# Distance attention on one Trainium2 core: who spreads the first two tiles of keys of a new pair of batches

## The reference, cut to what matters

```
q, k, v = (x @ W.T + b).reshape(B, S, 16, 8)          # B=8, S=512
distance = pos_q[:, None] - pos_q[None, :]
pos_emb = dist_emb[MAX_POS - 1 + distance]
scores  = einsum('bqhd,bkhd->bhqk', q, k) / sqrt(8)
scores += einsum('bqhd,qkd->bhqk', q, pos_emb)
scores += einsum('bkhd,qkd->bhqk', k, pos_emb)
ctx = einsum('bhqk,bkhd->bqhd', softmax(scores), v)
```

## Time and profile before

| | |
|---|---|
| median of 3 runs | 4081.83 us (4081.24 to 4086.81) |
| the profiled execution | 4118.69 us, its span 4117.0 us |
| distance attention in the profile | about 2570 to 3750 us of the span |
| PE busy | 3405.0 us (83%) |
| DVE busy | 3335.7 us (81%) |
| ACT busy | 2876.1 us (70%) |
| POOL busy | 1125.8 us (27%) |

### The profile page before, as it was taken

The page is one execution under the profiler, slowest core; times in us unless marked ns, Lnnn a source line. Parts: engine busy times, 40 slices in busy tenths (PEclk is TensorE's granted clock), DMA queues, the critical chain, the costliest instruction groups (busy, mean ns, idle before and its releaser), DMA issues. The chain is left out here.

```text
span 4117.0 us, 71499 instructions
## 1 busy us (share of the span) xinstructions
PE 3405.0 (83%) x27092; PEld 2097.7 (51%) x27092; DVE 3335.7 (81%) x4520; ACT 2876.1 (70%) x2433; POOL 1125.8 (27%) x983
## 2 busy tenths in 40 slices
PE   3899999999999999999947963688988898898890
PEld 2233333333333333333335861587887887887790
DVE  7999999999999999999937445668777787876662
ACT  3999999999999999999903323466666675664430
POOL 2121111221122111112100543534333334330235
PEclk8899999999999999999977986799999999997995
DMA  5000000000000000000031224411213113111022
GB/s 157 7 13 6 13 13 6 13 13 13 6 13 13 6 13 13 6 13 13 5 107 67 56 56 139 97 25 33 39 25 48 31 25 54 18 25 68 26 63 67
DMA packets 237595, 146.44 MB, mean 36 GB/s; under 512 B 147105, under 2 KB 220417, under 8 KB 236833
## 3 DMA queue, kind: packets, MB, share of 16 engines
q1 hardware_dynamic: 228640, 125.03, 12.6%
q0 software_dynamic: 8704, 17.84, 1.8%
HBM read 90.73 MB, written 52.10 MB: 35 GB/s over the span
## 5 line engine op out<-in xcount | busy, mean ns | idle before, releaser
L698 PE MATMUL psA<-wave,diag 128*128 128x512 f32 x3072 | 1439.9, 620 | 137.5 <-DVE score L854 89.4
L766 ACT ACTIVATE wave<-wave 128x2048 f32<-128x2048 int32 x640 | 1181.1, 1904 | 3.5 <-DVE wave L841 2.1
L698 PEld LDWEIGHTS psA<-wave,diag 128*128 128x128 f32 x3072 | 582.3, 196 | 895.5 <-issue 696.8
L635 POOL TENSOR_TENSOR diag<-ident,par 128x128 f32<-128x128 f32 x384 | 291.6, 785 | 1422.7 <-PE psA L698 1422.7
L816 DVE TENSOR_SCALAR wave<-s,par 128x2048 int32<-128x2048 int32 x480 | 611.1, 1273 | 0.0
L841 DVE TENSOR_SCALAR wave<-wave 128x2048 int32<-128x2048 int32 x512 | 608.4, 1212 | 0.0
L1729 POOL COPY kb<-ks 48x1024 bf16<-48x1024 bf16 x160 | 319.0, 1994 | 570.4 <-PE psR L1789 380.7
L1870 ACT COPY r<-psR 128x1024 f32<-128x1024 f32 x320 | 310.9, 1026 | 155.0 <-PE psR L1789 154.9
L731 ACT ACTIVATE s<-psS,par 128x1024 int32<-128x1024 f32 x256 | 282.6, 1104 | 121.9 <-PE psS L661 121.9
L854 DVE SCALAR_TENSOR_TENSOR score<-wave,par,psA 128x1024 f32<-128x1024 f32 x256 | 317.3, 1269 | 36.9 <-PE psA L698 36.9
L1879 ACT ACTIVATE W<-psR 128x1024 f32<-128x1024 f32 x256 | 249.4, 1024 | 132.3 <-PE psR L1814 132.3
(11 more groups left out here) (259 smaller groups left out, 4461.5 us busy)
## 6 DMA issues: line engine op xcount, KB each, us to landing
ks<-kb_parts SPq DMA_DIRECT2D x56, 384.0 KB, 6.2
qs<-qb_parts SPq DMA_DIRECT2D x32, 384.0 KB, 6.2
ys<-f_ys SPq DMA_DIRECT2D x36, 256.0 KB
wave_out<-og SPq DMA_DIRECT2D x33, 256.0 KB, 2.1
o<-wave_out SPq DMA_DIRECT2D x8, 1024.0 KB, 5.2
qp<-qa_parts SPq DMA_DIRECT2D x32, 192.0 KB, 3.5
kp<-ka_parts SPq DMA_DIRECT2D x32, 192.0 KB, 4.0
f_wu<-in_w_up SPq DMA_DIRECT2D x2, 2048.0 KB, 9.5
```

The lines of the kernel that those rows point to most:

```text
L635: ins = pool.tensor_tensor(diag[:, h % 2, f, :], ident[:], par[:, u, 1, h * NF + f:h * NF + f + 1] .to_broadcast((P, P)), ALU.mult)
L698: mm = pe.matmul(psA[:, kt, :], diag[:, h % 2, f, :], wave[:, h % 2, f, kt * L:(kt + 1) * L], start=(f == 0), stop=(f == PE_F - 1), skip_g ...
L766: act.activation(wave[:, h % 2, f, :], angle[:, h % 2, f, :], ACT.Sin, scale=float(TWO_PI / 2.0 ** 32)).then_inc(sine, 1)
```

## The change

At the three boundaries the keys of the first two units (u = 16, 17, 32, 33, 48, 49) are no longer spread by POOL. They leave `spread_steps`, and with it `k_order`. Instead ACT copies one quarter of the tile behind each of eight exponentials of the last query tile of the old pair: keys of the first unit behind e2, e3, e4, e5, keys of the second behind e8, e9, e10, e11. Ahead of the first quarter of each tile ACT waits for the tile's transfer and for the last r2 that read the buffer. PE waits on a new semaphore for these tiles. All other spreads stay on POOL, four copies each as before, only written through the common helper `quarter`.

```diff
-                for v in (u + QT, u + QT + 1):
-                    if v in k_spreads:
-                        yield "k", v
...
+    new_keys = [u for u in range(QT * QT, NU) if u % (QT * QT) < 2]
+    quarters = {(u // QT - 1, 2 + 6 * (u % QT) + n): (u, n) for u in new_keys for n in range(4)}
...
+        new_kb_ready = sem(c, "new_kb_ready")
...
+        def quarter(dst, src, n):
+            half, odd = divmod(n, 2)
+            pairs = slice(half * PAIRS // 2, (half + 1) * PAIRS // 2)
+            rows = slice(odd * ODD, odd * ODD + NR)
+            return (dst[rows, pairs, odd, :],
+                    src[rows, :, :].rearrange("r h (n two) -> r n h two", two=2)[:, pairs, :, odd])
...
-                    if u in k_spreads and k % 2 == 0:
+                    if u in new_keys and k % 2 == 0:
+                        pe.wait_ge(new_kb_ready, 4 * new_keys.index(u) + k + 2)
+                    elif u in k_spreads and k % 2 == 0:
                         pe.wait_ge(kb_ready, 4 * k_order.index(u) + k + 2)
...
+            def spread_new(u, n):
+                if n == 0:
+                    act.wait_ge(ks_loaded[ks_of(u)], 32 * k_landed(u))
+                    act.wait_ge(filled, fill["r2", k_spreads[u], CH - 1] + 1)
+                act.copy(*quarter(kb[:, kb_of(u), :, :, :], ks[:, ks_of(u), :, :], n)).then_inc(new_kb_ready, 1)
...
                 elif kind == "e":
                     weigh(i, k)
+                    if (i, k) in quarters:
+                        spread_new(*quarters[i, k])
```

More of the change, by code:

```diff
@@ L1723, in _ @@
         def _(pool):
[L1725 to L1732, removed]
             def spread_q(q):
@@ L1738, in spread_q @@
                         pool.wait_ge(filled, fill["r1", q * QT - 1, 2 * half + 1] + 1)
-                    spread(qb, qs[:, q % 2, :, :], half, qb_ready)
+                    for n in (2 * half, 2 * half + 1):
+                        pool.tensor_copy(*quarter(qb, qs[:, q % 2, :, :], n)).then_inc(qb_ready, 1)
             def spread_k(u):
@@ L1744, in spread_k @@
                     pool.wait_ge(filled, fill["r2", k_spreads[u], CH - 1] + 1)
-                for half in range(2):
-                    spread(kb[:, kb_of(u), :, :, :], ks[:, ks_of(u), :, :], half, kb_ready)
+                for n in range(4):
+                    pool.tensor_copy(*quarter(kb[:, kb_of(u), :, :, :], ks[:, ks_of(u), :, :], n)).then_inc(kb_ready, 1)
             pool.memset(kb[:, 0, :, :, :], 0.0).then_inc(zeroed, 1)
```

## The result

The changed kernel is slower. Over 18 runs its median is 4095.29 us (4083.51 to 4106.44) against 4083.07 us (4074.29 to 4093.75) for the kernel before; the ratio is 1.003, with a 95% interval from 1.0021 to 1.0038. I had said 4058.8 us, 0.57% faster. The two whole spans of the profiles (4117.0 us before, 4090.0 us now) say nothing on the change: the profiled execution of the kernel before took 4118.69 us, 35.6 us over that median, and outside the distance attention it was 31.7 us longer than the profiled one of the changed kernel. I compare boundary tiles, from one spread of queries to the next.

A forecast was written before the change was run, and what follows sets the result against it. DVE's subtractions under POOL's copies were taken to set the boundary tiles' time. 3 x (-10.44 regained + 2.75 for ACT's quarters) = -23.1 us off the median of 4081.8 gave 4058.8 us, range 4050 to 4070.

The forecast's parts named there:

- e8: Exponential on ACT, filled by PE beforehand; the second tile's first quarter follows it, and the layout starts it at 2742.36.
- e11: Exponential on ACT, filled by PE beforehand; the second tile's last quarter follows it, and the layout starts it at 2749.38.
- The price of a quarter: One strided key copy on ACT: 0.95 us taken, lower bound 0.9, upper bound POOL's 1.99 for the same pattern.
- Idle time, ring and hand-over: ACT's 3.52 us idle in the first tile, the ring's room before PE's e7, and 0.2 us from ACT to PE.
- the layout: ACT's row laid out anew with the quarters, against PE's fill times; at 0.95 us a quarter r2[3] starts 2.75 us late.
- e7: PE's fill for an exponential, where the first tile's cost was read: 0 as forecast, 2.7 us at 2.0 us a quarter.
- In short: 4 quarters less 1.05 us of slack. After that nothing is later: Second tile's cost on PE: r2[3] 2.75 us late, all that follows moving by the same amount.
- e13: PE's fill for an exponential, waiting for ACT to take e11; forecast to start 1.73 us late.
- e14: PE's fill for an exponential after r2[3]; forecast as ready, with no lateness beyond that of r2[3].
- e15: PE's last fill for an exponential in the unit, after e14; forecast with no lateness beyond that of r2[3].
- The sum at 2.0 us: Both tiles' costs together if a quarter takes 2.0 us: 10.6 us a boundary.
- The rival: Strided read on ACT: at 1.99 us a quarter costs eat the gain, slower by over 0.2% from 2.33; chance 0.04.

The follow-up runs named there:

- The probe: Changed kernel plus a block behind the distance attention where ACT, POOL and DVE each make the same 48 x 1024 copy in several forms; 4270.06 us, single run.
- the second tile alone: Changed kernel with only ACT's four quarters for the second tile, the first unit's new keys never spread; ratio 0.9975 to the kernel before.
- The runs with one tile: Changed kernel with ACT's four quarters for only the first or only the second tile, the other never spread; ratios 0.996 and 0.9975 to the kernel before.

## Why the prediction was wrong, step by step

- **What bounds the boundary tiles: right.** POOL's copies stretched DVE's subtractions. With the copies gone the mean is 480 ns, and the tiles without any spread of new keys were 32.3 us shorter, where I had 31.3 from the subtractions alone and 3.3 of clock as perhaps.
- **The price of a quarter: wrong, and it decides.** The step that failed is "I take 0.95 us for a quarter". It took 2.00, over the 1.2 us that I had named as the sign of being wrong. I priced by the engine, from a stepped read of PSUM and a contiguous read of SBUF, and put POOL's 1.99 us for the very same pattern at the far end as if it were a slow engine's. The second of these rows was no support at all: 1904 - 1026 = 878, and 1904 less 878 gives back the 1026 that I had put in. The probe shows that ACT and POOL cost nearly the same for the same pattern (1.91 and 1.88 us), and that the step of the read in SBUF makes both 1.8 times as dear. Of the rows that I had, the one with the same operands was the nearest.
- **Idle time, ring and hand-over: right at their price.** At 1.04 us a quarter PE was 3.4 us late where the layout gives 3.1, and the kernel was 19.0 (medians) to 20.8 us (ratio) faster where I had said 23.1. At 2.0 us the first tile cost 3.7 us and not 2.7, since I stopped at e7 and ACT, still full, held e8 as well.
- **"In short: 4 quarters less 1.05 us of slack. After that nothing is later": wrong at the real price.** The text priced a wait of PE at its length. At 2 us a quarter PE is busy 2.2 of the 5 us around e13 and r2[3], its clock falls to 0.50, and it does r2[3], v5 and some or all of e14 and e15 at about half pace: 2.6 us at the first boundary of the changed kernel, 2.0 at the second, 2.9 with the second tile alone. The stall of the kernel before had a low clock too (0.65 and 0.67 from 2870 to 2880 us), but there PE was waiting for DVE in any case.
- **The sum at 2.0 us: wrong by itself.** The text has 10.6 us a boundary, but its own terms give 2.7 + (8.0 - 1.05) = 9.65 us (and 6.15, not 6.6, at 1.5 us). The runs with one tile give 3.7 us for the first, 0.7 more where the clock falls behind e7, and 7.0 for the second; with the 2.6 us at the end that is 14.0 of the 14.1 us measured. That the 10.6 lay near 3.7 + 7.0 was luck.
- **The rival.** At 1.99 us I had the costs "eat the gain", with a loss beyond 0.2% only from 2.33 us on. With the lower clock the point of decision lies lower: at 2.00 us the kernel is 0.3% slower. Without it the two tiles would by this sum have cost 10.7 us, about what DVE got back, so the price of the quarter ate the gain and the clock made the loss. The mechanism of that rival is what happened; its chance of 0.04 and its threshold were wrong.
- **Waits and transfers: right.** PE never waited for the new keys, ACT never for a transfer.

## What to carry to other kernels

Price a moved copy by its access pattern in the memory where it lies, before the engine: if another engine already does this very copy, its time is the first estimate. A wait put on PE can cost more than its length: if the granted clock falls with it and PE has work of its own right behind, that work takes up to 1.8 times as long (v5 1.90 us for 1.06). Do not count on either outcome, since of two waits of 1.9 us here one had it and one had not. When one engine is relieved because two of them collide, look for the one whose idle time comes after its own deadline (here DVE behind its last subtraction), and keep the other one out of that time with one wait.

## What the runs showed of the hardware

- A copy of 48 x 1024 bf16 takes 1.04 us on ACT and 1.03 on POOL when it reads contiguously or every second element, and 1.91 and 1.88 us when it reads one element every 256 bytes.
- Writing bf16 in steps of 128 bytes takes 4.75 us on ACT, 4.73 on POOL and 2.44 on DVE for the same 1024 elements, with either of the two reads tried (contiguous, and every second element); writing runs of 64 bytes with gaps costs nothing (1.04 us).
- DVE makes the stepped read in 1.01 us and the contiguous one in 0.42, so it is 1.9 times as fast as ACT or POOL at the first and 2.5 times at the second; reading every second element costs it 0.68 us. Its stepped copy and POOL's, run side by side, hold each other up (2.79 us at most for one of DVE's, 2.77 for one of POOL's).
